# Order of two waits before the product and before its result, and a state turned in blocks of 32 and 96 columns

## The reference

```python
def _derivative(q, p, drive, coupling, bias):
    i_couple = jnp.tanh(q) @ coupling.T
    dq = q - q ** 3 / 3.0 - p + drive + i_couple + bias
    dp = EPSILON * (q + ALPHA - BETA * p)
    return (dq, dp)

def _rk4_step(q, p, drive, coupling, bias):
    dq1, dp1 = _derivative(q, p, drive, coupling, bias)
    dq2, dp2 = _derivative(q + 0.5 * DT * dq1, p + 0.5 * DT * dp1, drive, coupling, bias)
    dq3, dp3 = _derivative(q + 0.5 * DT * dq2, p + 0.5 * DT * dp2, drive, coupling, bias)
    dq4, dp4 = _derivative(q + DT * dq3, p + DT * dp3, drive, coupling, bias)
    ...
(_, _), q_trace_tbn = jax.lax.scan(scan_fn, (q0, p0), drive_tbn)
...
x = x + _L0_ffn_ref(_L0_cond2_ref(cond, cond, x, coupling, bias), w_gate, w_up, w_down, up_index, down_index)
```

## Time and profile before

| | us |
|---|---|
| median of 3 runs (1556.99 to 1558.44) | 1557.22 |
| the profiled execution | 1557.68 |
| its span in the trace | 1555.9 |
| first L1571 | 959.5 |
| last L1571 | 1515.0 |

### The profile page before, as it was taken

One profiled execution on the slowest core, in us unless ns is written; L12 is line 12 of the kernel. 1 busy time (PEld: TensorE's weight loads), 2 busy tenths in 40 slices (PEclk: granted clock), 3 DMA queues, 4 the chain that ended last, 5 costly groups with the idle time before them and its releaser, 6 DMA issues. The chain is left out here.

```text
span 1555.9 us, 45967 instructions
## 1 busy us (share of the span) xinstructions
PE 1476.6 (95%) x16653; PEld 928.6 (60%) x16694; DVE 1069.0 (69%) x3434; ACT 586.6 (38%) x1918; POOL 479.6 (31%) x676
## 2 busy tenths in 40 slices
PE   6999999998989999999999999999999999999995
PEld 2333333334866757586767665766666666666662
DVE  1676767775665545455655552578999999899987
ACT  2444445543021110202010213455555565655552
POOL 0212121111211202020202110245566555655662
PEclk9999999998989999999999999999999999999998
DMA  8121112113500000001000104211111111111112
GB/s 315 45 52 49 46 49 64 59 49 104 89 1 1 27 7 20 14 13 27 0 27 0 28 2 154 92 32 38 35 37 34 49 44 36 36 36 36 36 33 55
DMA packets 91427, 72.68 MB, mean 47 GB/s; under 512 B 32856, under 2 KB 83032, under 8 KB 90456
## 3 DMA queue, kind: packets, MB, share of 16 engines
q1 hardware_dynamic: 71544, 59.09, 12.9%
q10 hardware_dynamic: 18048, 6.89, 1.7%
q0 software_dynamic: 1760, 5.77, 1.3%
HBM read 54.76 MB, written 16.94 MB: 46 GB/s over the span
## 5 line engine op out<-in xcount | busy, mean ns | idle before, releaser
L896 PE MATMUL ps<-mem 128*32 128x128 f32 x8192 | 277.3, 275 | 25.3 <-ACT mem L1175 17.1
L896 PEld LDWEIGHTS ps<-mem 128*32 128x32 f32 x8192 | 209.6, 109 | 98.4 <-ACT mem L1175 69.5
L583 POOL TENSOR_TENSOR mem<-mem 128x256 f32<-128x256 f32 x128 | 92.8, 725 | 438.4 <-DVE mem L1428 438.4
L788 PE MATMUL ps<-mem 128*128 128x256 f32 x1024 | 222.3, 379 | 0.0
L788 PEld LDWEIGHTS ps<-mem 128*128 128x128 f32 x1024 | 193.9, 190 | 26.0
L686 PE MATMUL ps<-mem 128*32 128x384 f32 x2048 | 179.9, 493 | 6.3 <-ACT mem L1107 3.9
L698 PE MATMUL ps<-mem 128*32 128x384 f32 x2048 | 178.1, 488 | 3.0 <-DVE mem L1348 2.4
L758 PE MATMUL ps<-mem 128*128 128x512 f32 x384 | 168.7, 592 | 0.0
L1132 ACT ACTIVATE mem<-mem 128x512 f32<-128x512 f32 x32 | 19.7, 630 | 386.8 <-DVE mem L1460 386.8
L1175 ACT ACTIVATE mem<-mem 128x64 f32<-128x64 f32 x512 | 109.9, 250 | 89.0 <-DVE mem L1520 83.4
L886 PE MATMUL ps<-mem 128*128 128x128 f32 x768 | 136.6, 301 | 1.6
(11 more groups left out here) (159 smaller groups left out, 2159.2 us busy)
## 6 DMA issues: line engine op xcount, KB each, us to landing
mem<-x_scr SPq DMA_DIRECT2D x127, 64.0 KB, 1.8
mem<-in_xT SPq DMA_DIRECT2D x64, 64.0 KB, 1.8
mem<-in_Wq SPq DMA_DIRECT2D x1, 4096.0 KB, 12.4
mem<-in_Wo SPq DMA_DIRECT2D x1, 4096.0 KB, 22.2
q_scr<-mem SPq DMA_DIRECT2D x64, 64.0 KB, 1.6
mem<-q_scr SPq DMA_DIRECT2D x64, 64.0 KB, 1.9
out<-mem SPq DMA_DIRECT2D x64, 64.0 KB, 1.6
mem<-in_W_ih SPq DMA_DIRECT2D x1, 3072.0 KB, 10.7
```

The costliest lines, as they stand in the source:

```text
L583: pool.tensor_tensor(one, one, turned[h % 2].rearrange("p (b t) -> p b t", t=T), ALU.add).then_inc(qr_done, 1)
L788: mm = pe.matmul(ps[:, h % Q_BANKS, 0:BLK], wq[:, c, h * DH:(h + 1) * DH], xnb[:, c, :], start=(c == 0), stop=(c == NC - 1))
L896: mm = pe.matmul(ps[32 * j:32 * j + 32, st % 2, 0:P], thT[:, c, :], ct[:, c, j * P:(j + 1) * P], start=False, stop=(c == NC - 1), skip_gro ...
```

## The change

Six edits, all in the scan:

1. DVE, before L1571: the two waits are written in the other order. The wait for the product (rk_mm) is now carried by the instruction, the one for ebuf (rk_e) by the sequencer in front of it.
2. DVE, the seed of stage 0: from the third step on it no longer waits for rk_drive, and the wait for rk_p stays with the instruction. The wait for rk_drive is put on an earlier seed, that of stage 2 of the step before.
3. PE, products of stages 1 to 3: no wait for rk_seed (`mix_into` has waited for it).
4. PE, products of stage 0 in the written-out groups: the wait for rk_th is written first. In the loop its order stays.
5. The state of stages 1 to 3 is turned (DVE) and put through tanh (ACT) as one block of 32 columns and one of 96, that of stage 0 as two of 64 as before (`TURNED`).
6. PE waits for the second block behind the 4 matmuls of the first chunk in stages 1 to 3, and behind 8 in stage 0.

```diff
+TURNED = (((0, 2), (2, 4)),) + (((0, 1), (1, 4)),) * 3
+TURNED_STEP = sum(len(TURNED[st]) for st in range(4))
+def turned_through(t, st, i):
+    return TURNED_STEP * t + sum(len(TURNED[k]) for k in range(st)) + i + 1
...
-            def stage(t, s, st):
+            def stage(t, s, st, written_out):
                 n = 4 * t + st
-                pe.wait_ge(rk_seed, n + 1)
+                if st == 0 and not written_out:
+                    pe.wait_ge(rk_seed, n + 1)
+                firsts = [lo for lo, _ in TURNED[st]]
                 for c in range(NC):
-                    if c % 2 == 0:
-                        pe.wait_ge(rk_th, 2 * n + c // 2 + 1)
+                    if c in firsts:
+                        pe.wait_ge(rk_th, turned_through(t, st, firsts.index(c)))
+                    if c == 0 and st == 0 and written_out:
+                        pe.wait_ge(rk_seed, n + 1)
...
-                for half in range(2):
-                    act.wait_ge(rk_qT, 2 * n + half + 1)
-                    act.activation(thT[:, 2 * half:2 * half + 2, :], qsT[:, 2 * half:2 * half + 2, :], ACT.Tanh).then_inc(rk_th, 1)
+                for i, (lo, hi) in enumerate(TURNED[st]):
+                    act.wait_ge(rk_qT, turned_through(t, st, i))
+                    act.activation(thT[:, lo:hi, :], qsT[:, lo:hi, :], ACT.Tanh).then_inc(rk_th, 1)
...
+            def turned_piece(src, lo, hi):
+                dve.transpose(qsT[:, lo:hi, :].rearrange("p c b -> p (c b)"), src[:, 32 * lo:32 * hi]).then_inc(rk_qT, 1)
+            def state_turned(src, st):
+                for lo, hi in TURNED[st]:
+                    turned_piece(src, lo, hi)
...
                 if st == 0:
-                    dve.wait_ge(rk_drive, t + 1)
                     wait_if(dve, rk_p, t)
+                    if t < 2:
+                        dve.wait_ge(rk_drive, t + 1)
...
                 else:
+                    if st == 2 and 0 < t < T - 1:
+                        dve.wait_ge(rk_drive, t + 2)
...
+                dve.wait_ge(rk_mm, n + 1)
                 dve.wait_ge(rk_e, n + 1)
-                dve.wait_ge(rk_mm, n + 1)
```

More of the change, by code:

```diff
@@ L977, in group @@
                         pe.wait_ge(x1_done, PRIMED + PAIRS * NBLK - 1)
-                    stage(4 * g + k // 4 + (nought if isinstance(g, int) else 0), k // 4, k % 4)
+                    stage(4 * g + k // 4 + (nought if isinstance(g, int) else 0), k // 4, k % 4, isinstance(g, int))
                     slot(k, tile)
@@ L1516, in _ @@
             dve.tensor_scalar(pn[1], pn[1], -ALPHA / BETA, None, ALU.add).then_inc(rk_start, 1)
-            def turned_half(src, half):
-                dve.transpose(qsT[:, 2 * half:2 * half + 2, :].rearrange("p c b -> p (c b)"), src[:, half * 64:half * 64 + 64]).then_inc(rk_qT, 1)
-            def state_turned(src):
-                turned_half(src, 0)
-                turned_half(src, 1)
-            state_turned(qn[3])
+            def turned_piece(src, lo, hi):
[3 more added lines that the diff above has]
+                    turned_piece(src, lo, hi)
+            state_turned(qn[3], 0)
             part_residual(6, xres[:, 0, :], 1)
@@ L1577, in stage @@
                 if st < 3:
-                    state_turned(dst)
+                    state_turned(dst, st + 1)
                 else:
                     if not end:
-                        turned_half(dst, 0)
+                        turned_piece(dst, *TURNED[0][0])
                         seed(t + 1, (s + 1) % 4, 0)
-                        turned_half(dst, 1)
+                        turned_piece(dst, *TURNED[0][1])
                     wait_if(dve, q_wr[s], PRIMED + 16 * g)
```

## The result

| | us |
|---|---|
| median before, 4 runs (1556.99 to 1558.44) | 1557.13 |
| median after, 4 runs (1538.95 to 1545.57) | 1541.49 |
| ratio, 95% interval | 0.990 (0.9877 to 0.9923) |
| the profiled execution after, its span | 1542.53, 1540.6 |
| first and last L1587 | 961.04, 1500.28 |

The kernel got 15.6 us faster; the forecast was 1541.7. L1571 is now L1587, its event in front L1585, the turning L1533, square L1180, tanh L1188, product L909, `mix_into` L895, L1170 is L1183, L1561 and L1547 are L1577 and L1563, the seed of stage 0 L1559, L1536 is L1549. POOL's L592, L596, L602 are L601, L605, L611; PE's filling L775, L912, L921, L931, L968 is L784, L925, L934, L944, L981.

A forecast was written before the change was run, and what follows sets the result against it. It took the chain from state through tanh and product to the next state as the bound, with filling of PE, DVE or POOL next. Loop 8.8 plus written-out 6.7 gave 15.5 us, so 1541.7 us; forecast 1538 to 1545, range 1537 to 1549.5.

The forecast's parts named there:

- The chain of a bare slot: Stages 1 to 3, slots with little filling: 0.07 less from the DVE wait, 0.06 from the split; 2.13 becomes 2.00 in loop.
- Loop groups: Twelve groups, counted slot by slot with what is late next: 0.72 to 0.73 us saved a group, 8.8 us in all.
- Slot 10: Loop slot counted as bare, like slots 3 and 7: 0.13 us saved a group.
- Slots 13, 14, 15 and 0: Loop slots bounded by POOL's chain L592, L596, L607, L614, L602 before slot 0's seed: 0.11 us saved for the four.
- Written-out groups: 64 slots outside the loop, split by the filling ahead of the product: 0, 2.6 and 4.1 us, sum 6.7 us.
- PE is next after 0.10 to 0.14: 22 written-out slots with one to three filling pieces: PE's filling bounds after that gain; 0.12 each, 2.6 us.
- The stall stays: Group 0, slot 9: the 1.2 us stall was expected to remain.
- 1: Order of waits is free, only the split's 0.06 counts: 6.3 us saved, 1550.9 us; chance 0.08.
- 2: Split brings nothing, ACT holds tanh until the square ends: 11.9 us saved, 1545.3 us; chance 0.12.
- rival 3: POOL's and DVE's unchanged work takes back 0.39 a loop group and a like share elsewhere: 8.2 left, 1549.0; chance 0.10.
- 4: Slower: PE waits inside the product for the block of 96; at 0.155 delay it costs 22, 1564 us; chance 0.03.
- 5: More: PE's and DVE's filling also closes up in slots put at 0; 6 us more, 1536 us; chance 0.07.

The follow-up runs named there:

- E: Kernel after with the second L616 of POOL's filling moved from slot 14 to slot 15, behind L605 and L611; 1542.95 us, scan 537.92 us.
- B: Kernel before with only the two waits before L1571 put in the new order; 1546.89 us, scan 546.91 us.

## Why the prediction was right, point by point

**The chain of a bare slot.** Right: 2.13 - 0.07 - 0.06 = 2.00 was measured as 2.00 in slots 3 and 7 and 1.99 in slot 15. That the stage's DVE instruction gains what ACT's carried wait had shown in the recurrent stage held: 67 ns there in the median, 67 here.

**Loop groups**, forecast against measured, in us: slot 1 0.05 and 0.046; 2 none and none; 3 and 7 0.13 and 0.13; 4 0.05 and 0.057; 5 0.02 and 0.017; 6 0.05 and 0.047; 8 none and none; 9 0.02 and 0.009; 11 none and none. Three terms were off.

- *Slot 10*, forecast 0.13, measured 0.04. I called it bare, for in the rows of PE it had only four small matmuls ahead of the product. There was a fifth, the last piece of the down product: its record of PE is missing, its weight load is in the trace of before.

```profile
1260.03 0.39 PE L921 MATMUL ps<-mem 128*128 128x128 bf16 x4
1260.19 0.10 PEld L968 LDWEIGHTS ps<-mem 128*128 128x128 bf16 x1
...
1260.60 1.08 PE L896 MATMUL ps<-mem 128*32 128x128 f32 x32 [0.19 <-ACT mem L1175]
```

DOWN_SLOTS says the same: one matmul behind slot 9. In after the record is there, at 0.63, and the product starts 0.31 behind it. A view of weight loads beside matmuls would have shown it.
- *Slots 13, 14, 15 and 0*, forecast 0.11, measured 0.093 (20 - 16 + 130 - 41 ns). The mechanism was right: POOL's chain sets the four, and of slot 15's gain of 0.13 slots 0 and 14 pay back 0.06. The size holds by two sides: E shows that another 0.10 lay in the one L616.
- *Slot 12*, forecast 0.03, measured 0.055: DVE had, it seems, more room there than I had given it; no run asks that.

The twelve groups gave 8.22 us, forecast 8.8 (its terms add up to 0.72 a group, so rather 8.6). The medians make 0.619 of 0.685 a group, 7.4 us in all. The other 0.8 is the long slots of before named under the result, which the prediction didn't know of. So what it did name fell short of 8.8 by 1.4 us, not by 0.6.

**Written-out groups**, forecast 6.7 with the stall left in: the four groups together went from 141.48 to 133.45, by 8.03. Of that 1.35 is the slot of the stall (1.22 for the stall, 0.13 as its like), which leaves 6.68. By kind: 0.07 in the seven slots behind five pieces (forecast 0), 2.75 in those with fewer pieces (2.6), 3.86 in the others (4.1). Group 0 shows how the parts cover each other: its common slots take 2.21 before, 2.15 with the DVE edit alone, and 2.09 as soon as two of the three are in, with or without the third, for then L784 sets the product. The step "PE is next after 0.10 to 0.14" was right (0.125). *The stall stays* was wrong.

**The total.** 15.5 forecast for the scan, 16.25 measured: + 1.35 for the slot of the stall, - 0.6 for the loop. That the two lie so close is in part luck: without that slot and the long slots of before, 14.1 was gained of 15.5. The stretches outside gave 1.0 back, 1.54 later at the start and 0.52 shorter at the end.

**What the three edits are worth** depends on what else is in: undone one at a time they cost 5.6, 2.4 and 1.2, together 9.2 of 16.2. The rest is where two of them open the same slot, and the seed's edit (2), which no run undid alone; nor were edits 3 and 4 told apart. The prediction's sums by slot deal with that; a sum by edits would not.

**Rivals.** 1 fell by B (8.6 us from an order alone). 2 fell by slot 7: tanh starts at 0.57, so ACT takes it up before the square's end. 3 is true in part. Of the split, 0.061 in four slots of twelve groups would be 2.9 us, and 0.8 of them arrive in the loop; the 2.1 that are given back are nearly half of the 4.7 (0.39 a group) that rival 3 took there for all edits. The DVE edit alone gives back what slot 15 gains too (B: 0.07 less there, 0.05 and 0.02 more in 0 and 14), which the prediction had in its count. But slots 3 and 7 keep their 0.13, and slot 8 stays as long as it was. 4 needs 0.05 of delay to begin, and the run with the square between shows that it does. 5: slots 2, 8 and 11, which I had put at 0, stayed at 0; the one slot that gave more is that of the stall, 1.35 of its 6.

## What to carry to other kernels

Of two waits on one instruction, let it carry the one that comes last, and leave the early one to the sequencer: here 0.07 us a stage on DVE and 0.09 on PE, 8.6 us of the scan for one swapped pair of lines. Look at what stands behind the loop too: a move that made the scan 1.3 us shorter put what follows it 1.5 us later. Work out a gain slot by slot, with what is late next in each, and don't add edits that open the same slot. Where a slot seems bare, count its instructions in the code too, and in weight loads: a missing record cost the prediction 0.09 us in each loop group.

## What the runs showed of the hardware

- A wait carried by a DVE instruction lets it start 67 ns behind the modelled end of the last matmul (23 ns behind the semaphore's update), one held by the sequencer's event 137 ns (93 ns); on PE the two are 0.29 and 0.38 behind tanh's start. A wait that is long over costs nothing on the sequencer: TensorE's loop groups take 405.61 us with it and 405.79 without it in stages 1 to 3.
- A product whose second block comes late stops in the middle: it gets longer by the delay over 0.05 us, and by 0.025 more.
- A product of float32 behind bf16 filling starts 0.31 behind the start of the last matmul of 512 columns, and 0.24 behind the last of 352.
- One product in group 0 stopped for 0.84 to 1.11 us, with nothing awaited, in the three kernels with PE's old order of waits, and in none of the ten with the new. Its cause is open.
- The same program took 1538.95 to 1545.57 us in four executions, with mean granted clocks of 0.989 to 0.982. The scan is at 1.00 in every trace; what lies outside it took 998.2 to 1002.1 us in the eight kernels whose stretches outside are alike.
